# Order of Silu, Exp and Ln in the front stage of a three-layer Mamba block

## Chip, cores and metric

One core of a Trainium2 chip. The metric is the device time of one execution of the whole program in microseconds, the median of three runs.

## What is computed

A tower of token embedding with attention, a delta-rule attention block, two mixtures of experts and, between them, three Mamba layers beside an LSTM. The change is in the Mamba layers alone:

```
xz = einsum('bld,ed->ble', x, wi); xin, z = split(xz, 2)
u = silu(cb + conv4(xin, cw))
xdbl = einsum('blc,ec->ble', u, xpw)
dt_in, Bc, Cc = xdbl[..., :32], xdbl[..., 32:48], xdbl[..., 48:]
dt = softplus(einsum('blr,cr->blc', dt_in, dw) + db)
A = -exp(Alog)
h = exp(dt_t * A) * h + (dt_t * u_t) * B_t      # scan over 128 steps
y = (h . C_t + u * Dp) * silu(z);  m = layernorm(m + y @ wo)
```

There are 16 sequences of 128 tokens, 256 channels and 16 states.

## The kernel before

The program is a row of stages, each a block in which the engines run their own lists of instructions and wait on semaphores; a barrier stands at the end of a block. Each Mamba layer has two blocks: `mamba_front_stage`, which makes u, gate, dt, dtu = dt * u and the B and C rows, and `mamba_scan_stage`, which runs 64 turns of decay, scan and accumulation (in layers 1 and 2 with one LSTM step in each turn). When a block ends, POOL alone clears its semaphores (`close_semaphores`, L39 to L45) before it starts on the next.

The front stage works on four groups of 512 columns (4 sequences). 256 channels are two halves of 128 partitions, so most tiles of a group are 128 partitions by 2x512. The order in each engine's list is written out by hand:

- PE: `turn` (transpose), `channels_in` and `gates_in` (input projection), `project` (x_proj, L1567), `step_in` (dt projection, one half at a time through one PSUM bank, L1574).
- ACT: `normal`, `turned`, `gate` (Silu from PSUM, L1357), `channels` (Silu, L1361), `projected` (two copies, L1365 and L1366), `step_input` (dt with its bias, L1370), and `logarithm` (L1372 on), which makes log(1 + exp(-|x|)): Abs L1375, Exp L1377, the small Exp of A_log with group 0, L1379, and Ln L1383. A change of function that needs another table is preceded by an ACT_TABLE_LOAD, which the compiler puts in.
- DVE: `statistics`, `mean_shift`, `convolve`, `split` (B and C into bf16 parts, L1462, CAST L1464, L1466), and `step_size`, five instructions of 128x1024: w = (e + 1) - 1 (L1472), e = w - e (L1475), l = (w > 0) * l (L1476), l = l - e (L1479), dt = max(x, 0) + l (L1481). w is what 1 + e keeps of e, so the sum is softplus with the lost bits of e added. In the first layer some one-off scalings for the LSTM (L1508 to L1514) stand ahead of the last step size, in all layers the sign of A (L1517).
- POOL: `inverse_root` and `step_times_input`, dtu = dt * u, one instruction of 128x1024 for each group (L1324), which waits for dt.
- SP: the C rows go to DRAM.

The tile `ln` and the tile `conv` have two buffers each, used by groups in turn; e lies in tile y, w in tile dtu.

```
dve.wait_ge(s["w_done"], g + 1)
dve.wait_ge(s["ln_done"], g + 1)
nc.vector.tensor_tensor(e, w, e, ALU.subtract).then_inc(s["diff_done"], 1)
```

Of the kernel before, what the change touches and what calls it, by code (L numbers as in the profile page):

```python
# [9 lines left out]
ALU = mybir.AluOpType  # L10
ACT = mybir.ActivationFunctionType
# [5 lines left out]
GROUPS = 4  # L17
# [1256 lines left out]
def mamba_front_stage(nc, io, m, z, r, layer):  # L1274
# [5 lines left out]
                            "e_done w_done ln_done a_exp a_done diff_done masked_done t_done dt_done dtu_done")  # L1280
    with ExitStack() as mem:
# [14 lines left out]
        def cols(g):  # L1296
            return slice(g * GT, (g + 1) * GT)
# [5 lines left out]
        with nc.Block() as block:  # L1303
# [12 lines left out]
            @block.gpsimd  # L1316
            def _(pool):
                def inverse_root(g):
                    pool.wait_ge(s["var_done"], g + 1)
                    nc.gpsimd.tensor_tensor(root[:, g, :], var[:, g, :], m.neg_half[:, 0:GS], ALU.pow).then_inc(s["root_done"], 1)  # L1320

                def step_times_input(g):
                    pool.wait_ge(s["dt_done"], g + 1)
                    nc.gpsimd.tensor_tensor(z["dtu"][:, :, cols(g)], z["dt"][:, :, cols(g)], z["u"][:, :, cols(g)], ALU.mult).then_inc(s["dtu_done"], 1)  # L1324

                for g in range(GROUPS):
                    inverse_root(g)
                if first:
                    nc.gpsimd.memset(r["hs"][:, 0:1, :], 0.0)
                    nc.gpsimd.memset(r["cell"][:, :], 0.0).then_inc(s["cleared"], 1)  # L1330
                    pool.wait_ge(s["cleared"], 1)
                for g in range(GROUPS):
                    step_times_input(g)
                pool.wait_ge(s["dtu_done"], GROUPS)

            @block.scalar
            def _(act):
# [34 lines left out]
                def logarithm(g):  # L1372
                    e = z["y"][:, :, cols(g)]
                    act.wait_ge(s["x_done"], HALVES * (g + 1))
                    nc.scalar.activation(e, z["dt"][:, :, cols(g)], ACT.Abs).then_inc(s["abs_done"], 1)  # L1375
                    act.wait_ge(s["abs_done"], g + 1)
                    nc.scalar.activation(e, e, ACT.Exp, scale=-1.0).then_inc(s["e_done"], 1)  # L1377
                    if g == 0:
                        nc.scalar.activation(z["a"][:, :, :], z["a_log"][:, :, :], ACT.Exp).then_inc(s["a_exp"], 1)  # L1379
                    act.wait_ge(s["e_done"], g + 1)  # L1380
                    if g >= 2:
                        act.wait_ge(s["dt_done"], g - 1)
                    nc.scalar.activation(ln[:, g % 2], e, ACT.Ln, bias=m.ones_col[:, 0:1]).then_inc(s["ln_done"], 1)  # L1383
# [21 lines left out]
                logarithm(0)  # L1405
                channels(2)
                gate(3)
                step_input(1, 0)
                channels(3)
                step_input(1, 1)  # L1410
                projected(2)
# [3 lines left out]
                step_input(2, 1)  # L1415
                logarithm(2)
                step_input(3, 0)
                step_input(3, 1)
                logarithm(3)

            @block.vector
            def _(dve):
# [45 lines left out]
                def step_size(g):  # L1468

                    e, w, l, x = z["y"][:, :, cols(g)], z["dtu"][:, :, cols(g)], ln[:, g % 2], z["dt"][:, :, cols(g)]  # L1470
                    dve.wait_ge(s["e_done"], g + 1)
                    nc.vector.tensor_scalar(w, e, 1.0, -1.0, ALU.add, ALU.add).then_inc(s["w_done"], 1)  # L1472
                    dve.wait_ge(s["w_done"], g + 1)
                    dve.wait_ge(s["ln_done"], g + 1)
                    nc.vector.tensor_tensor(e, w, e, ALU.subtract).then_inc(s["diff_done"], 1)  # L1475
                    nc.vector.scalar_tensor_tensor(out=l, in0=w, scalar=0.0, in1=l, op0=ALU.is_gt, op1=ALU.mult).then_inc(s["masked_done"], 1)  # L1476
                    dve.wait_ge(s["masked_done"], g + 1)
                    dve.wait_ge(s["diff_done"], g + 1)
                    nc.vector.tensor_tensor(l, l, e, ALU.subtract).then_inc(s["t_done"], 1)  # L1479
                    dve.wait_ge(s["t_done"], g + 1)  # L1480
                    nc.vector.scalar_tensor_tensor(out=x, in0=x, scalar=0.0, in1=l, op0=ALU.max, op1=ALU.add).then_inc(s["dt_done"], 1)  # L1481
# [18 lines left out]
                convolve(3)  # L1500
                step_size(0)
                split(2)
                step_size(1)
                split(3)
                step_size(2)
# [11 lines left out]
                nc.vector.tensor_scalar(z["a"][:, :, :], z["a"][:, :, :], -1.0, None, ALU.mult).then_inc(s["a_done"], 1)  # L1517
                step_size(3)
                dve.wait_ge(s["a_done"], 1)
# [7 lines left out]
            def _(pe):  # L1527
# [69 lines left out]
                channels_in(3)  # L1597
                gates_in(3)
                step_in(1, 0)
                project(2)  # L1600
# [1643 lines left out]
```

## Time and profile before

| | us |
|---|---|
| median of 3 runs (lowest, highest) | 2222.15 (2221.86, 2230.19) |
| the profiled execution, its own time | 2218.03 |
| its span | 2216.2 |
| busy: PE / DVE / ACT / POOL | 1795.8 / 1491.5 / 1081.9 / 1121.8 |
| front stages, from first to last work | about 1006 to 1084, 1301 to 1388, 1628 to 1707 |
| scan stages | about 1084 to 1301, 1388 to 1628, 1707 to 1945 |

The span is the time from the first to the last instruction of the profiled execution; all times of the trace count from its start. The busy times are sums over the whole program, so what an engine bounds in one stage is not read from them. In a timeline each row is one instruction, or several alike in a row (x2), with its start, its duration and, in brackets, how long its engine sat idle before it and what it waited for. From the start of one row to the start of the next is what an instruction costs its engine: it may be a little less than the duration, since the next one overlaps, or a little more, where the next one waits for its result.

### The profile page before, as it was taken

The page shows a single profiled execution, that of the slowest core. Times are in us where ns is not written, and L with a number is a line of the kernel's source. Part 1 is how long each engine was busy: PE and PEld are TensorE (multiplying, and loading weights), DVE is VectorE, ACT ScalarE, POOL GpSimd, SP SyncE. Part 2 cuts the span into 40 slices and gives each one's busy share as a digit, 9 for nine tenths or more (in the row PEclk, how much of TensorE's full clock was granted, in tenths as well). Part 3 has the DMA queues.
Part 4 walks back from the last instruction along what each step waited for, and adds up shares of the span by engine and source line. Part 5 has one row for each costly group of instructions (what it writes and reads, how often), then busy time and mean ns, then how long its engine had stood idle before and what let it go on. Part 6 is the DMA issues. An engine that isn't in the chain of part 4 may idle for free. (4 is left out here: it accounts for less than half of the span.)

```text
span 2216.2 us, 39566 instructions
## 1 busy us (share of the span) xinstructions
PE 1795.8 (81%) x13962; PEld 1146.5 (52%) x13962; DVE 1491.5 (67%) x2798; ACT 1081.9 (49%) x2732; POOL 1121.8 (51%) x1094
## 2 busy tenths in 40 slices
PE   7986799999976789766477785999984999975990
PEld 4554467767665569742122241566641666643550
DVE  4657877777623412247799968899967899955552
ACT  3662256666643424325666647555546455541110
POOL 4100656555580220051499951899922899924005
PEclk9997899999987579988699997899995899987995
DMA  8000111111111048410132200332201222203662
GB/s 298 14 1 8 43 33 35 29 40 40 40 33 27 19 136 220 135 34 19 44 86 81 81 24 3 79 84 77 76 3 23 68 77 77 68 17 94 193 180 66
DMA packets 196552, 149.91 MB, mean 68 GB/s; under 512 B 93393, under 2 KB 155687, under 8 KB 194838
## 3 DMA queue, kind: packets, MB, share of 16 engines
q1 hardware_dynamic: 191766, 138.74, 22.5%
q0 software_dynamic: 4608, 8.86, 1.4%
q8 instruction: 104, 1.70, 0.3%
q14 instruction: 74, 0.61, 0.1%
HBM read 108.93 MB, written 39.19 MB: 67 GB/s over the span
## 5 line engine op out<-in xcount | busy, mean ns | idle before, releaser
L1685 POOL TENSOR_TENSOR mc_hc<-mc_states,mc_c_sb 128x1024 f32<-128x1024 f32 x192 | 451.4, 2351 | 40.5 <-DVE mc_states L1778 29.5
L1778 DVE TENSOR_TENSOR_SCAN mc_states<-psum,mc_dbu 128x512 f32<-128x512 f32 x384 | 459.9, 1217 | 13.0 <-POOL mc_dbu L1675 7.9
L1816 PE MATMUL psum<-mc_hc,ident 128*128 128x512 f32 x768 | 421.3, 644 | 49.4 <-POOL mc_hc L1685 46.7
L1696 ACT ACTIVATE psum<-dt,a 128x508 f32<-128x508 f32 x384 | 261.3, 686 | 18.3 <-DVE mc_states L1778 17.0
L815 POOL TENSOR_TENSOR fw_tmp<-zeros 128x30 f32<-128x30 f32 (+14 forms) x240 | 127.0, 529 | 201.7 <-DMA zeros<-fw_blocks 183.5
L1675 POOL TENSOR_TENSOR mc_dbu<-dtu,mc_b_sb 128x384 f32<-128x384 f32 x192 | 191.4, 998 | 10.6 <-remote 7.0
L1816 PEld LDWEIGHTS psum<-mc_hc,ident 128*128 128x128 f32 x768 | 122.6, 193 | 108.4 <-POOL mc_hc L1685 68.1
L853 ACT ACTIVATE fw_U<-psum 32x128 f32<-32x128 f32 x440 | 118.1, 269 | 97.1 <-PE psum L1114 49.9
L1764 DVE TENSOR_TENSOR mc_dbu<-psum,dtu 128x640 f32<-128x640 f32 x192 | 154.0, 802 | 7.0 <-PE psum L1796 6.7
L1703 ACT ACTIVATE mc_b_sb<-psum 128x192 f32<-128x192 f32 x192 | 63.5, 331 | 170.6 <-PE psum L1802 170.1
L819 POOL TENSOR_TENSOR zeros<-zeros,fw_tmp 128x30 f32<-128x30 f32 (+14 forms) x240 | 131.3, 547 | 18.8
L2001 POOL DMA_INDIRECT c_y<-slots_y,slots x32 | 30.3, 948 | 152.7 <-issue 152.7
L2001 POOL DMA_INDIRECT f_y<-slots_y,slots x32 | 31.2, 974 | 149.5 <-issue 149.5
L1324 POOL TENSOR_TENSOR dtu<-dt,u 128x1024 f32<-128x1024 f32 x12 | 28.1, 2342 | 152.5 <-DVE dt L1481 152.5
L1096 PE MATMUL psum<-fw_qkT 64*128 64x128 f32 x1024 | 79.7, 298 | 27.3 <-DVE fw_A L1025 26.4
L2450 ACT ACTIVATE e_up<-psum,e_b 128x256 f32<-128x256 f32 x128 | 56.7, 474 | 84.3 <-PE psum L2495 84.3
L1096 PEld LDWEIGHTS psum<-fw_qkT 64*128 64x128 f32 x1024 | 66.7, 199 | 41.3 <-DVE fw_A L1025 29.4
L1848 PEld LDWEIGHTS psum<-ls_parts,mc_half_ident 128*128 128x128 f32 x256 | 49.4, 197 | 72.9 <-DVE ls_parts L1770 56.2
L3012 ACT ACTIVATE e_act<-psum 64x256 f32<-64x256 f32 x64 | 24.2, 377 | 125.4 <-PE psum L3057 125.4
L1834 PE MATMUL psum<-ls_hs,ls_whh 64*64 64x16 f32 x2048 | 85.3, 212 | 0.0
L1802 PE MATMUL psum<-bc,select 96*128 96x192 bf16 x192 | 48.9, 255 | 44.9 <-PEq L1303 43.7
L2460 DVE TENSOR_SCALAR e_xT<-psum,x_gb 128x256 f32<-128x256 f32 x32 | 17.4, 544 | 94.8 <-PE psum L2488 94.8
(439 smaller groups left out, 4120.0 us busy)
## 6 DMA issues: line engine op xcount, KB each, us to landing
mc_c_sb<-c_rows SPq DMA_DIRECT2D x192, 256.0 KB, 3.2
e_w<-in_L_ffn_ew SPq DMA_DIRECT2D x64, 256.0 KB, 3.2
slots_x<-zeros SPq DMA_DIRECT2D x12, 1024.0 KB, 14.5
e_x<-slots_x SPq DMA_DIRECT2D x96, 128.0 KB, 2.3
slots_y<-e_y SPq DMA_DIRECT2D x96, 128.0 KB, 2.0
e_w<-in_L_ffn_w SPq DMA_DIRECT2D x64, 128.0 KB, 2.2
fw_blocks<-fw_A SPq DMA_DIRECT2D x128, 32.0 KB, 1.7
zeros<-fw_blocks SPq DMA_DIRECT2D x8, 512.0 KB, 3.7
```

Of the source, the lines that this page charges most:

```text
L815: nc.gpsimd.tensor_tensor(part, z[:, u + 1:BLK, u:u + 1].to_broadcast([P, rows, u]), z[:, u:u + 1, 0:u].to_broadcast([P, rows, u]), ALU.mu ...
L819: nc.gpsimd.tensor_tensor(z[:, u + 1:BLK, 0:u], z[:, u + 1:BLK, 0:u], part, ALU.subtract).then_inc(s["subtracted"], 1)
L853: last = nc.scalar.activation(U[BLK * i:BLK * (i + 1), 2 * r:2 * r + 2, :], RU8[place(i, r), 2 * r:2 * r + 2, :], ACT.Copy)
L1096: last = nc.tensor.matmul(S[h % 2][:, h // 2, :], qkT[lo:lo + DH, 1, h // 2, :], qkT[lo:lo + DH, k, h // 2, :], start=True, stop=True)
L1675: nc.gpsimd.tensor_tensor(dbu[:, k % 2, :, SPLIT:GT], z["dtu"][:, :, c * GT + SPLIT:(c + 1) * GT], b_sb[:, k % 2, :].unsqueeze(1).to_broad ...
L1685: nc.gpsimd.tensor_tensor(hc[:, k % 2], states[:, k % 2], c_sb[:, k % AHEAD, :].unsqueeze(1).to_broadcast([P, HALVES, GT]), ALU.mult).then ...
L1696: nc.scalar.activation(decay4[:, f, :, 1:P], z["dt"][:, f, cols].rearrange("p (b t) -> p b t", b=GS)[:, :, 1:P], ACT.Exp, scale=z["a"][:, ...
L1703: nc.scalar.activation(b_sb[:, k % 2, :], rest_ps, ACT.Copy).then_inc(s["b_copied"], 1)
L1764: nc.vector.tensor_tensor(dbu[:, k % 2, :, 0:SPLIT], b_ps[k % 2][:, 0:SPLIT].unsqueeze(1).to_broadcast([P, HALVES, SPLIT]), z["dtu"][:, :, ...
L1778: nc.vector.tensor_tensor_scan(out=states[:, k % 2, f, :], data0=decay_ps[:, f, :], data1=dbu[:, k % 2, f, :], initial=0.0, op0=ALU.mult, ...
L1816: last = nc.tensor.matmul(y_ps[:, f, :], m.ident, hc[:, k % 2, f, :], start=(n == 0), stop=(n == NSTATE - 1), skip_group_check=True)
L1834: last = nc.tensor.matmul(step_ps[rows, q * BATCH:(q + 1) * BATCH], r["whh"][rows, q, rows], hs[rows, first_step + k, :], start=False, sto ...
```

## The change

On ACT the function `logarithm` is cut into `magnitude` (Abs), `exponential` and `logarithm` (Ln alone). The Silus of groups 2 and 3 and the copies of group 2 stand ahead of the first Exp. Exp of groups 0 and 1 follow one another, with the small Exp behind, then Ln of 0 and 1. Groups 2 and 3 keep Exp and Ln each. At the end a table load for the scan's Exp is issued.

On DVE `step_size` is cut into `step_base` (w, w - e, max(x, 0) - (w - e)), which needs Exp alone, and `step_size` (mask of Ln and the sum). The sum is taken in another order; w - e goes to the tile conv, so it also waits for the last Silu that reads it. On POOL the last product is cut: POOL does the first half, DVE the second, with a wait for dt. On PE `project(2)` moves ahead of `gates_in(3)`.

```
-                def logarithm(g):
+                def magnitude(g):
+                    act.wait_ge(s["x_done"], HALVES * (g + 1))
+                    nc.scalar.activation(z["y"][:, :, cols(g)], z["dt"][:, :, cols(g)], ACT.Abs).then_inc(s["abs_done"], 1)
+
+                def exponential(g):
                     e = z["y"][:, :, cols(g)]
-                    act.wait_ge(s["x_done"], HALVES * (g + 1))
-                    nc.scalar.activation(e, z["dt"][:, :, cols(g)], ACT.Abs).then_inc(s["abs_done"], 1)
                     act.wait_ge(s["abs_done"], g + 1)
                     nc.scalar.activation(e, e, ACT.Exp, scale=-1.0).then_inc(s["e_done"], 1)
-                    if g == 0:
-                        nc.scalar.activation(z["a"][:, :, :], z["a_log"][:, :, :], ACT.Exp).then_inc(s["a_exp"], 1)
+
+                def logarithm(g):
                     act.wait_ge(s["e_done"], g + 1)
...
                 step_input(0, 1)
-                logarithm(0)
+                magnitude(0)
                 channels(2)
+                projected(2)
                 gate(3)
                 step_input(1, 0)
                 channels(3)
+                exponential(0)
                 step_input(1, 1)
-                projected(2)
+                magnitude(1)
+                exponential(1)
+                nc.scalar.activation(z["a"][:, :, :], z["a_log"][:, :, :], ACT.Exp).then_inc(s["a_exp"], 1)
+                logarithm(0)
                 logarithm(1)
                 step_input(2, 0)
                 projected(3)
                 step_input(2, 1)
+                magnitude(2)
+                exponential(2)
                 logarithm(2)
                 step_input(3, 0)
                 step_input(3, 1)
+                magnitude(3)
+                exponential(3)
                 logarithm(3)
+                nc.scalar.preload_act_table_set("exp_and_others")
...
+                def step_base(g):
+                    e, w, x = z["y"][:, :, cols(g)], z["dtu"][:, :, cols(g)], z["dt"][:, :, cols(g)]
+                    diff = conv[:, g % 2].rearrange("p f j c -> p f (j c)")
                     dve.wait_ge(s["e_done"], g + 1)
                     nc.vector.tensor_scalar(w, e, 1.0, -1.0, ALU.add, ALU.add).then_inc(s["w_done"], 1)
                     dve.wait_ge(s["w_done"], g + 1)
+                    dve.wait_ge(s["u_done"], GROUPS)
+                    if g >= 2:
+                        dve.wait_ge(s["base_done"], g - 1)
+                    nc.vector.tensor_tensor(diff, w, e, ALU.subtract).then_inc(s["diff_done"], 1)
+                    dve.wait_ge(s["diff_done"], g + 1)
+                    nc.vector.scalar_tensor_tensor(out=x, in0=x, scalar=0.0, in1=diff, op0=ALU.max, op1=ALU.subtract).then_inc(s["base_done"], 1)
+
+                def step_size(g):
+                    w, l, x = z["dtu"][:, :, cols(g)], ln[:, g % 2], z["dt"][:, :, cols(g)]
                     dve.wait_ge(s["ln_done"], g + 1)
-                    nc.vector.tensor_tensor(e, w, e, ALU.subtract).then_inc(s["diff_done"], 1)
                     nc.vector.scalar_tensor_tensor(out=l, in0=w, scalar=0.0, in1=l, op0=ALU.is_gt, op1=ALU.mult).then_inc(s["masked_done"], 1)
                     dve.wait_ge(s["masked_done"], g + 1)
-                    dve.wait_ge(s["diff_done"], g + 1)
-                    nc.vector.tensor_tensor(l, l, e, ALU.subtract).then_inc(s["t_done"], 1)
-                    dve.wait_ge(s["t_done"], g + 1)
-                    nc.vector.scalar_tensor_tensor(out=x, in0=x, scalar=0.0, in1=l, op0=ALU.max, op1=ALU.add).then_inc(s["dt_done"], 1)
+                    dve.wait_ge(s["base_done"], g + 1)
+                    nc.vector.tensor_tensor(x, x, l, ALU.add).then_inc(s["dt_done"], 1)
+
+                def last_step_times_input():
+                    dve.wait_ge(s["dt_done"], GROUPS)
+                    c = cols(GROUPS - 1)
+                    nc.vector.tensor_tensor(z["dtu"][:, 1, c], z["dt"][:, 1, c], z["u"][:, 1, c], ALU.mult).then_inc(s["dtu_last"], 1)
...
                 convolve(3)
+                split(2)
+                step_base(0)
                 step_size(0)
-                split(2)
+                step_base(1)
                 step_size(1)
                 split(3)
+                step_base(2)
                 step_size(2)
...
+                step_base(3)
                 step_size(3)
+                last_step_times_input()
...
                 channels_in(3)
+                project(2)
                 gates_in(3)
                 step_in(1, 0)
-                project(2)
```

On ACT, first layer, from the Abs of group 0 (y is the tile of e, mf_ln the tile of Ln, u takes the Silu of the convolution, zeros and bc the two copies). Before:

```order
L1375 ACTIVATE y<-dt 128x2x512
L1377 ACT_TABLE_LOAD
L1377 ACTIVATE y<-y 128x2x512
L1379 ACTIVATE a<-ma_log 128x32
L1383 ACT_TABLE_LOAD
L1383 ACTIVATE mf_ln<-y,ones_col 128x1024
L1361 ACT_TABLE_LOAD
L1361 ACTIVATE u<-mf_conv 128x2x512
L1357 ACTIVATE gate<-psum 128x512 x2
L1370 ACTIVATE dt<-psum,mdb 128x512
L1361 ACTIVATE u<-mf_conv 128x2x512
L1370 ACTIVATE dt<-psum,mdb 128x512
```

And now:

```order
L1376 ACTIVATE y<-dt 128x2x512
L1363 ACTIVATE u<-mf_conv 128x2x512
L1367 ACTIVATE zeros<-psum 64x512
L1368 ACTIVATE bc<-psum 32x512
L1359 ACTIVATE gate<-psum 128x512 x2
L1372 ACTIVATE dt<-psum,mdb 128x512
L1363 ACTIVATE u<-mf_conv 128x2x512
L1381 ACT_TABLE_LOAD
L1381 ACTIVATE y<-y 128x2x512
L1372 ACTIVATE dt<-psum,mdb 128x512
L1376 ACTIVATE y<-dt 128x2x512
L1381 ACTIVATE y<-y 128x2x512
```

The three loads between Abs and the Silus of groups 2 and 3 are now one, behind both Silus, and the second Exp follows the first without a load.

On DVE, first layer, from the step size of group 0 to that of group 1 (dtu holds w, mf_conv now the difference). Before:

```order
L1472 TENSOR_SCALAR dtu<-y 128x2x512
L1475 TENSOR_TENSOR y<-dtu,y 128x2x512
L1476 SCALAR_TENSOR_TENSOR mf_ln<-dtu,mf_ln 128x1024
L1479 TENSOR_TENSOR mf_ln<-mf_ln,y 128x1024
L1481 SCALAR_TENSOR_TENSOR dt<-dt,mf_ln 128x2x512
L1462 TENSOR_TENSOR mf_rest<-psum,bc 32x512
L1464 CAST bc<-mf_rest 32x512
L1466 TENSOR_TENSOR bc<-mf_rest,bc 32x512
L1472 TENSOR_SCALAR dtu<-y 128x2x512
L1475 TENSOR_TENSOR y<-dtu,y 128x2x512
```

And now:

```order
L1476 TENSOR_TENSOR mf_rest<-psum,bc 32x512
L1478 CAST bc<-mf_rest 32x512
L1480 TENSOR_TENSOR bc<-mf_rest,bc 32x512
L1488 TENSOR_SCALAR dtu<-y 128x2x512
L1493 TENSOR_TENSOR mf_conv<-dtu,y 128x1024
L1495 SCALAR_TENSOR_TENSOR dt<-dt,mf_conv 128x2x512
L1500 SCALAR_TENSOR_TENSOR mf_ln<-dtu,mf_ln 128x1024
L1503 TENSOR_TENSOR dt<-dt,mf_ln 128x2x512
L1488 TENSOR_SCALAR dtu<-y 128x2x512
L1493 TENSOR_TENSOR mf_conv<-dtu,y 128x1024
L1495 SCALAR_TENSOR_TENSOR dt<-dt,mf_conv 128x2x512
```

The split of group 2 (mf_rest, bc) stands ahead of the first step size instead of behind it, and the step sizes of groups 0 and 1 follow one another with nothing between them.

## Rows read from the trace of the kernel before

**Rows 1.** The page, costliest groups: line engine op tiles | busy us, mean ns | idle us before
```profile
L1324 POOL TENSOR_TENSOR dtu<-dt,u 128x1024 f32<-128x1024 f32 x12 | 28.1, 2342 | 152.5 <-DVE dt L1481 152.5
```

**Rows 2.** Timeline of ACT, first layer: start us, us, engine line op, tiles, shapes [idle before]
```profile
1036.12 0.69 ACT L1370 ACTIVATE dt<-psum,mdb 128x512 f32<-128x512 f32 x1
1036.83 1.06 ACT L1375 ACTIVATE y<-dt 128x1024 f32<-128x1024 f32 x1
1037.91 1.28 ACT L1377 ACT_TABLE_LOAD   x1
1039.20 1.06 ACT L1377 ACTIVATE y<-y 128x1024 f32<-128x1024 f32 x1
...
1040.40 1.28 ACT L1383 ACT_TABLE_LOAD   x1
1041.69 1.15 ACT L1383 ACTIVATE mf_ln<-y,ones_col 128x1024 f32<-128x1024 f32 x1
1042.86 1.28 ACT L1361 ACT_TABLE_LOAD   x1
...
1045.11 1.07 ACT L1357 ACTIVATE gate<-psum 128x512 f32<-128x512 f32 x2
...
1075.04 1.15 ACT L1383 ACTIVATE mf_ln<-y,ones_col 128x1024 f32<-128x1024 f32 x1
```

**Rows 3.** Timeline of DVE, first layer, step size of group 0
```profile
1044.16 0.68 DVE L1472 TENSOR_SCALAR dtu<-y 128x1024 f32<-128x1024 f32 x1
1044.88 1.23 DVE L1475 TENSOR_TENSOR y<-dtu,y 128x1024 f32<-128x1024 f32 x1
1046.02 1.22 DVE L1476 SCALAR_TENSOR_TENSOR mf_ln<-dtu,mf_ln 128x1024 f32<-128x1024 f32 x1
1047.27 1.22 DVE L1479 TENSOR_TENSOR mf_ln<-mf_ln,y 128x1024 f32<-128x1024 f32 x1
1048.53 1.23 DVE L1481 SCALAR_TENSOR_TENSOR dt<-dt,mf_ln 128x1024 f32<-128x1024 f32 x1
```

**Rows 4.** The same timeline at the end of the stage, DVE and POOL
```profile
1079.94 1.23 DVE L1481 SCALAR_TENSOR_TENSOR dt<-dt,mf_ln 128x1024 f32<-128x1024 f32 x1
...
1081.25 2.34 POOL L1324 TENSOR_TENSOR dtu<-dt,u 128x1024 f32<-128x1024 f32 x1 [7.05 <-DVE dt L1481]
```

**Rows 5.** Timeline of PE around x_proj; windows row: us, five engines busy, PEclk, DMA share, GB/s
```profile
1032.08 1.93 PE L1567 MATMUL psum<-u,mxw 128*64 128x512 f32 x4
...
1045.26 3.41 PE L1567 MATMUL psum<-u,mxw 128*64 128x512 f32 x4 [4.10 <-ACT u L1361]
...
1045.20:1071.00 25.80, 15.02 (x18) 3.38 (x18) 19.82 (x20) 20.31 (x25) 4.69 (x2) 0.63 0.01 3
```

**Rows 6.** Instructions by line over the span: duration ns min/median/max, first and last start
```profile
L1464 DVE CAST bc<-mf_rest x12: 414/414/1956, 1028.8 to 1686.8; 32x512 bf16<-32x512 f32 x12
...
L1510 DVE TENSOR_SCALAR ls_whh<-ls_whh x4: 214/219/2387, 1071.8 to 1074.3; 128x128 f32<-128x128 f32 x4
...
L1032 DVE TENSOR_TENSOR fw_qk<-fw_qk,fw_rz x32: 1224/1226/2453, 179.2 to 603.3; 128x1024 f32<-128x1024 f32 x32
```

**Rows 7.** Timeline of DVE and POOL, first layer, split of group 3 and the one-off scalings
```profile
1062.45 0.68 DVE L1462 TENSOR_TENSOR mf_rest<-psum,bc 32x512 f32<-32x512 f32 x1
...
1065.88 0.69 DVE L1472 TENSOR_SCALAR dtu<-y 128x1024 f32<-128x1024 f32 x1
...
1071.69 0.15 DVE L1508 TENSOR_TENSOR ls_bsum<-mf_bias 128x4 f32<-128x4 f32 x1
...
1074.80 0.68 DVE L1472 TENSOR_SCALAR dtu<-y 128x1024 f32<-128x1024 f32 x1
...
1062.50 2.34 POOL L1324 TENSOR_TENSOR dtu<-dt,u 128x1024 f32<-128x1024 f32 x1 [10.26 <-DVE dt L1481]
```

**Rows 8.** Timeline of POOL and DVE at the start of the first scan
```profile
1086.93 1.95 POOL L1675 TENSOR_TENSOR mc_dbu<-dtu,mc_b_sb 128x384 f32<-128x384 f32 x2 [3.35 <-remote]
...
1088.02 2.34 DVE L1778 TENSOR_TENSOR_SCAN mc_states<-psum,mc_dbu 128x512 f32<-128x512 f32 x2 [2.43 <-POOL mc_dbu L1675]
```

More of the change, by code:

```diff
@@ L1279, in mamba_front_stage @@
                             "in_mm gate_done taps conv_done u_done dbl_mm rows_done hi_done rest_done mid_done split_done rows_out dt_mm x_done abs_done "
-                            "e_done w_done ln_done a_exp a_done diff_done masked_done t_done dt_done dtu_done")
+                            "e_done w_done ln_done a_exp a_done diff_done base_done masked_done dt_done dtu_done dtu_last")
     with ExitStack() as mem:
@@ L1320, in inverse_root, with step_times_input @@
                     nc.gpsimd.tensor_tensor(root[:, g, :], var[:, g, :], m.neg_half[:, 0:GS], ALU.pow).then_inc(s["root_done"], 1)
-                def step_times_input(g):
+                def step_times_input(g, halves=range(HALVES)):
                     pool.wait_ge(s["dt_done"], g + 1)
-                    nc.gpsimd.tensor_tensor(z["dtu"][:, :, cols(g)], z["dt"][:, :, cols(g)], z["u"][:, :, cols(g)], ALU.mult).then_inc(s["dtu_done"], 1)
+                    f = slice(halves.start, halves.stop)
+                    nc.gpsimd.tensor_tensor(z["dtu"][:, f, cols(g)], z["dt"][:, f, cols(g)], z["u"][:, f, cols(g)], ALU.mult).then_inc(s["dtu_done"], 1)
                 for g in range(GROUPS):
@@ L1331, in _ @@
                     pool.wait_ge(s["cleared"], 1)
-                for g in range(GROUPS):
+                for g in range(GROUPS - 1):
                     step_times_input(g)
+                step_times_input(GROUPS - 1, range(1))
                 pool.wait_ge(s["dtu_done"], GROUPS)
@@ L1382, in logarithm @@
                         act.wait_ge(s["dt_done"], g - 1)
-                    nc.scalar.activation(ln[:, g % 2], e, ACT.Ln, bias=m.ones_col[:, 0:1]).then_inc(s["ln_done"], 1)
+                    nc.scalar.activation(ln[:, g % 2], z["y"][:, :, cols(g)], ACT.Ln, bias=m.ones_col[:, 0:1]).then_inc(s["ln_done"], 1)
                 if not first:
@@ L1466, in split @@
                     nc.vector.tensor_tensor(z["bc"][64:96, g, :], rest[:, g % 2, :], z["bc"][0:32, g, :], ALU.subtract).then_inc(s["split_done"], 1)
-                def step_size(g):
-                    e, w, l, x = z["y"][:, :, cols(g)], z["dtu"][:, :, cols(g)], ln[:, g % 2], z["dt"][:, :, cols(g)]
+                def step_base(g):
+                    e, w, x = z["y"][:, :, cols(g)], z["dtu"][:, :, cols(g)], z["dt"][:, :, cols(g)]
+                    diff = conv[:, g % 2].rearrange("p f j c -> p f (j c)")
                     dve.wait_ge(s["e_done"], g + 1)
@@ L1473, in step_size @@
                     dve.wait_ge(s["w_done"], g + 1)
+                    dve.wait_ge(s["u_done"], GROUPS)
[6 more added lines that the diff above has]
+                    w, l, x = z["dtu"][:, :, cols(g)], ln[:, g % 2], z["dt"][:, :, cols(g)]
                     dve.wait_ge(s["ln_done"], g + 1)
-                    nc.vector.tensor_tensor(e, w, e, ALU.subtract).then_inc(s["diff_done"], 1)
                     nc.vector.scalar_tensor_tensor(out=l, in0=w, scalar=0.0, in1=l, op0=ALU.is_gt, op1=ALU.mult).then_inc(s["masked_done"], 1)
                     dve.wait_ge(s["masked_done"], g + 1)
-                    dve.wait_ge(s["diff_done"], g + 1)
-                    nc.vector.tensor_tensor(l, l, e, ALU.subtract).then_inc(s["t_done"], 1)
-                    dve.wait_ge(s["t_done"], g + 1)
-                    nc.vector.scalar_tensor_tensor(out=x, in0=x, scalar=0.0, in1=l, op0=ALU.max, op1=ALU.add).then_inc(s["dt_done"], 1)
+                    dve.wait_ge(s["base_done"], g + 1)
[4 more added lines that the diff above has]
+                    nc.vector.tensor_tensor(z["dtu"][:, 1, c], z["dt"][:, 1, c], z["u"][:, 1, c], ALU.mult).then_inc(s["dtu_last"], 1)
+                    dve.wait_ge(s["dtu_last"], 1)
                 dve.wait_ge(m.front_loaded, FRONT_LOADS * (layer + 1))
```

## Prediction

> **What bounds the kernel now.** The change touches one stage that runs three times, the front of each recurrent layer, between the scans. Read first the page's group of the product dt times u on POOL [rows 1]: twelve instructions of 2.34 us, with 152.5 us of idle time in front of them, all of it waiting for dt from DVE. POOL is last in this stage and is fed by DVE. Then read the timeline of ACT, first layer [rows 2]. The reader is to see the table loads: Exp and Ln stand behind different tables, a Silu behind a third, and each load takes 1.28 us. From the start of Abs (1036.83) to Silu's load (1042.86) is 6.0 us, and the pattern is repeated for groups 1 to 3. Start-to-start steps I use: dt to Abs 0.71, Abs to the next 1.08, load to activation 1.29, Exp to the next 1.0 (its 1.06 less the overlap), Exp with the small Exp behind it 1.20. The last Ln starts at 1075.04 and ends at 1076.19. Then the timeline of DVE [rows 3]: a step size is five instructions of 1024 columns, started 0.72, 1.14, 1.25 and 1.26 us apart. Its second waits for Ln, so four instructions stand behind the last Ln. The last of them starts at 1079.94 and ends at 1081.17, and POOL's last product runs 1081.25 to 1083.59 [rows 4]. The end of the stage is therefore ACT's chain to the last Ln (1076.19), then 7.4 us of DVE and POOL. ACT is the bound, and DVE has slack in front of each Ln.
>
> Times below are those of the first layer; I price the other two by the same chain.
>
> **The change on ACT.** Three of the nine loads ahead of a stage's last Ln go: the Silus of groups 2 and 3 now stand ahead of the first Exp, and two Exps share one load, as do two Lns. The step sizes of group 0 come later for it. Up to 1037.91 nothing moves. Then, by steps from [rows 2]: Silu of group 2 ends at 1039.0. TensorE's x_proj for group 2 follows at once, 1.93 us if its clock is still up [rows 5], so ACT copies at 1041.1, does two copies and two gate Silus at 0.5 to 0.6 each (a pair of Silus takes 1.07), and waits for the dt matmul behind the gates' four matmuls (1040.95 + 1.93 + 1.0 = 1043.9). dt 0.6, Silu of group 3 at 1044.5, load at 1045.55, first Exp at 1046.85, dt at 1047.85, Abs at 1048.55, second Exp at 1049.65, load at 1050.85 behind the small Exp, first Ln at 1052.1. It ends at 1053.25; the masking on DVE starts 0.1 later, at 1053.35. Before it started at 1046.02, so the first step size is 7.3 us later. From there on ACT runs 3.3 us ahead of its old time: the last Ln ends at 1072.9.
>
> **The change on DVE.** Five instructions remain five, of the same sizes. Three of them (w, the difference, the base) no longer need Ln, and two follow it. If ACT stayed the bound, 1.25 + 1.22 us and half a product would stand behind the last Ln, and the end would be near 1076.7, 6.9 us earlier. But DVE has no slack left after 1053.35. It then owes five-instruction groups of 5.5 us (0.72 + 1.25 + 1.14 + 1.25 + 1.14) for groups 1 to 3, and the split of group 3.
>
> **Who blocks whom.** The question is what POOL's products of groups 0 to 2 do to a DVE that never rests. They have always run; what is new is that nothing covers them. The trace shows the price [rows 6]: the CAST of the split takes 0.414 us and once per layer or so 1.956, when a product runs beside it. One of four 128x128 scalings takes 2.387 instead of 0.22, and it was the second of four back to back: POOL had come in between two DVE instructions that were both ready. The multiplication at L1032, both inputs in SBUF, takes 1.224 or up to 2.453 while POOL works. L1462, with one input in PSUM, took 0.68 beside a product [rows 7]. So I take every DVE instruction with two SBUF inputs, and the fast one-input ones, as blocked for a whole product. That is a step beyond the rows, since no row has a SCALAR_TENSOR_TENSOR of this shape beside POOL. Bounds for one product: 0 (only the fast ones are blocked, and none is met) and 2.39. I take 2.2 for groups 0 and 2 in the later layers, since DVE's next instructions are all of the blocked kind.
>
> On this the Trainium skill (SBUF — State Buffer, Who interferes with whom) says that a Vector instruction with two SBUF inputs contends with a GpSimd instruction that reads SBUF, and that the second to issue blocks until the first is done. The trace agrees for TENSOR_TENSOR (1.224 to 2.453); for the two SCALAR_TENSOR_TENSOR of each group no row here shows it. By the page the sum is the one below; without it, it would be the first rival's.
>
> **The sum, first layer.** Masking 1053.35, dt of group 0 at 1054.6, w of group 1 at 1055.75. POOL asks at 1055.9 and gets in behind w: +2.15. dt of group 1 then at 1062.3. Split with its CAST blocked: 1.25 from dt, then 3.43 to the next w [rows 7] (1.89 without the block of 1.54); w of group 2 at 1067.0, dt at 1071.35. Then the one-off scalings of the first layer, 3.11 us, blocked as before, so w of group 3 at 1075.6, its dt at 1079.95 to 1081.2. The last product: DVE's half 0.68 (512 columns, as L1462), POOL's half 1.27 (on the line through 0.98 for 384 and 2.34 for 1024 columns [rows 1, 8]; half of 2.34 is the lower bound). Both have two SBUF inputs, so they come one behind the other: 1081.2 + 0.68 + 1.27 = 1083.15. Gain 0.4 us.
>
> **Second and third layer.** No one-off scalings, but the product of group 2 blocks two-input work of group 3: w at 1072.6, +2.2, dt at 1079.2 to 1080.4, halves to 1082.4. Gain 1.2 each. In the third the old end is some half a microsecond late, which I add: 1.7.
>
> **The load at the end of the stage.** It takes 1.28 off the scan's start on ACT. I cost it at nothing: the first scan waits for POOL's first mc_dbu (1086.93, ends 1087.9), and DVE starts at 1088.02 [rows 8]. POOL is late, 3.35 us idle, because it first clears the stage's 40 semaphores. There is one more now, at most 0.08 us (3.35 over 40), three times: -0.2. In front, the load stands behind the last Ln with 8 us to spare. The moved x_proj and the split of group 2 are hidden in the wait for the first Exp.
>
> Sum: 0.4 + 1.2 + 1.7 - 0.2 = **3.1 us faster**, against the profiled execution's 2218.0. The median of the three runs shown is 2222.15, 4 above it; I subtract from the median: **2219.0**. A measurement of this kernel can tell about 0.5% (11 us) from no change, so this is no change.
>
> **Rivals.**
> 1. *Only the fast one-input instructions are blocked.* For: the clearest blocked rows are of that kind. Against: L1032's 2.453. Then the first product costs nothing, and the last halves run side by side. First layer: dt of group 3 at 1077.75, end 1080.4, gain 3.2; in the others 4.0 if w of group 3 meets the product, 6.2 if not and ACT becomes the bound again. Sum 11.2 to 16, time 2206 to 2211. Chance 0.15.
> 2. *TensorE falls to its lower clock before x_proj of group 2; slower.* It does x_proj in 1.93 after steady work and in 3.41 after 4.1 us of idling, and was granted 0.63 of the full clock on average from 1045.2 to 1071 [rows 5], so part of that time at 1.2 and part at 2.4 GHz. In the new order x_proj, the gates and the dt matmul stand ahead of the first Exp. Slow, they cost 1.5 + 1.5 + 0.9 = 3.9 us on the way to the first Ln, and DVE pays all of it: 3 x 3.9 - 3.1 = 8.6 us slower, 2231, and beyond 0.5% only with another microsecond in each layer. It decides as soon as the first masking starts more than 1 us after 1053.35. Against: the gap before x_proj is only 0.6 us, since Silu comes at once. Chance 0.04.
> 3. *ACT stays the bound*, POOL's products slip into gaps: end near 1076.7 in each layer, 20 us, 2202. It needs 5 us of slack on DVE that I don't find. Chance 0.03.
>
> The forecast keeps 0.78; its own range, with a block of 0 to 2.4 us at each of the two new places, is 2213 to 2224. To hold the time 8 times in 10 I stretch down to part of rival 1: 2209 to 2224. Faster by over 0.5% (below 2211) has rivals 1 and 3, 0.17; slower by over 0.5% is the worse half of rival 2, 0.02; no change 0.81.
>
> **What would show it.** Right: the difference of group 1 takes 3.4 us instead of 1.23; the masking of group 0 starts 16 to 17 us after the Abs of group 0; from there no idle time on DVE until the end; ACT's last Ln ends 3 us earlier with 8 us of idling behind it; the halves lie one behind the other; the scan's first DVE instruction still waits for mc_dbu. Wrong: step-size instructions at 1.22 beside running products, DVE waiting for a later Ln, or x_proj of group 2 at 3.4 us.

## The result, and the profile after

The changed kernel takes 2218.22 us (median of 20 runs, 2212.54 to 2225.24), the kernel before 2223.43 in the same comparison (20 runs, 2217.94 to 2230.19). The ratio is 0.9973 with a 95% interval of 0.9962 to 0.9985: 3.3 to 8.4 us less, inside the 0.5% that the prediction called no change. The predicted 3.1 us would be a ratio of 0.9986, just outside that interval: the sign and the class were right, the size somewhat low. Ratios leave out executions over 1.5% longer than the fastest of the same kernel, in which TensorE's granted clock was lower; here there were none.

The profiled execution says the opposite at first sight: its span is 2218.6 us against 2216.2 before. So the change is read where it was made, as the time from the first Abs of a layer (ACT) to DVE's first instruction in that layer's scan stage. Layers are counted from 1 here and below, so the LSTM steps run in the scans of layers 2 and 3.

| us, layers 1 / 2 / 3 | front, first Abs to the scan stage | from there to the first scan |
|---|---|---|
| before | 47.28 / 47.26 / 47.73 | 3.90 / 4.19 / 4.19 |
| after | 46.42 / 45.43 / 45.43 | 4.27 / 4.27 / 4.27 |
| gain | 0.86 / 1.83 / 2.30 | -0.37 / -0.08 / -0.08 |

That is 4.99 us in front and 0.53 given back, 4.5 us in all, and it lies within the measured 3.3 to 8.4. What hides it in the profiled execution lies in stages with the same code in both kernels; a part below comes back to it.

POOL's group on the page, against [rows 1] (152.5 us idle, waiting for dt):

```profile
L1325 POOL TENSOR_TENSOR dtu<-dt,u 128x1024 f32<-128x1024 f32 (+1 forms) x12 | 28.4, 2366 | 147.3 <-DVE dt L1503 147.3
```

It is still the one that waits last, by 5.2 us less; the second form is the half. The timeline of ACT, first layer, answers to [rows 2]. This Abs starts at 1042.62 instead of 1036.83, so 5.79 us are to be taken off before times are compared.

```profile
1042.62 1.06 ACT L1376 ACTIVATE y<-dt 128x1024 f32<-128x1024 f32 x1
1043.58 1.04 ACT L1363 ACTIVATE u<-mf_conv 128x1024 f32<-128x1024 f32 x1
1046.64 0.59 ACT L1367 ACTIVATE zeros<-psum 64x512 f32<-64x512 f32 x1 [2.02 <-PE psum L1601]
...
1051.25 1.28 ACT L1381 ACT_TABLE_LOAD   x1
1052.55 1.06 ACT L1381 ACTIVATE y<-y 128x1024 f32<-128x1024 f32 x1
...
1057.79 2.19 ACT L1387 ACTIVATE mf_ln<-y,ones_col 128x1024 f32<-128x1024 f32 x2
...
1076.68 1.15 ACT L1387 ACTIVATE mf_ln<-y,ones_col 128x1024 f32<-128x1024 f32 x1
1077.84 1.28 ACT L1433 ACT_TABLE_LOAD   x1
1089.01 0.18 ACT L1752 ACTIVATE psum<-dt 128x8 f32<-128x8 f32 x1 [9.89 <-PEq L1303]
```

The reader is to see one load ahead of the first Exp, both first Lns as one row, and 9.89 us of idling behind the last load: ACT no longer sets the end. Its last Ln starts 34.06 us after the Abs, where it was 38.21. DVE and POOL in the same stretch, against [rows 3, 4, 7]:

```profile
1053.64 0.69 DVE L1488 TENSOR_SCALAR dtu<-y 128x1024 f32<-128x1024 f32 x1 [1.73 <-ACT y L1381]
1054.36 1.23 DVE L1493 TENSOR_TENSOR mf_conv<-dtu,y 128x1024 f32<-128x1024 f32 x1
1055.62 1.22 DVE L1495 SCALAR_TENSOR_TENSOR dt<-dt,mf_conv 128x1024 f32<-128x1024 f32 x1
1058.97 1.23 DVE L1500 SCALAR_TENSOR_TENSOR mf_ln<-dtu,mf_ln 128x1024 f32<-128x1024 f32 x1 [2.12 <-ACT mf_ln L1387]
...
1062.09 3.26 DVE L1493 TENSOR_TENSOR mf_conv<-dtu,y 128x1024 f32<-128x1024 f32 x1
...
1069.75 1.95 DVE L1478 CAST bc<-mf_rest 32x512 bf16<-32x512 f32 x1
...
1078.04 2.78 DVE L1542 TENSOR_SCALAR ls_whh<-ls_whh 128x128 f32<-128x128 f32 x4
...
1085.44 1.23 DVE L1503 TENSOR_TENSOR dt<-dt,mf_ln 128x1024 f32<-128x1024 f32 x1
1086.69 0.69 DVE L1509 TENSOR_TENSOR dtu<-dt,u 128x512 f32<-128x512 f32 x1
...
1061.60 2.66 POOL L1325 TENSOR_TENSOR dtu<-dt,u 128x1024 f32<-128x1024 f32 x1 [32.38 <-DVE dt L1503]
...
1086.74 1.77 POOL L1325 TENSOR_TENSOR dtu<-dt,u 128x512 f32<-128x512 f32 x1 [6.27 <-DVE dt L1503]
```

From the masking at 1058.97 to the half at 1086.69 no DVE row has idle time in front. Inside that stretch three rows are longer than their work: the difference of group 1 (3.26 for 1.23), the CAST (1.95 for 0.41) and the scalings (2.78 for four of 0.22), each beside a product of POOL. The last two rows of each engine show the halves one behind the other: POOL asks at 1086.74 while DVE's half runs until 1087.38, and ends at 1088.51, that is 1.13 after it. In layer 2 the difference of group 3 is the one blocked:

```profile
1382.14 3.24 DVE L1493 TENSOR_TENSOR mf_conv<-dtu,y 128x1024 f32<-128x1024 f32 x1
...
1395.66 1.22 DVE L1812 TENSOR_TENSOR_SCAN mc_states<-psum,mc_dbu 128x512 f32<-128x512 f32 x1 [1.29 <-POOL mc_dbu L1709]
```

The second row is the first scan: it waits for POOL's mc_dbu, as in [rows 8], and not for ACT.

### The profile page after: what moved, and what is told of

It is laid out like the page before. It is cut to its first block and busy times, and to the rows that moved or that the text cites. A ratio compares the mean times of both kernels' runs of the same rounds, so it can differ in the third digit from the quotient of the medians.

```text
span 2218.6 us, 39564 instructions
## 1 busy us (share of the span) xinstructions
PE 1797.8 (81%) x13962; PEld 1150.1 (52%) x13962; DVE 1499.9 (68%) x2801; ACT 1069.6 (48%) x2723; POOL 1121.1 (51%) x1094
## 5 line engine op out<-in xcount | busy, mean ns | idle before, releaser
L1325 POOL TENSOR_TENSOR dtu<-dt,u 128x1024 f32<-128x1024 f32 (+1 forms) x12 | 28.4, 2366 | 147.3 <-DVE dt L1503 147.3
```

## Experiments

Two questions were open. *Theory*: DVE's own work is the bound from the first masking on, and POOL's products block it, whichever instruction with two SBUF inputs is next. *Rival*: only the fast one-input instructions are blocked, or the wait for Ln still sets the end. The second question is which part of the change carries the gain. The three front times given with each run are those of one profiled execution; they repeat from kernel to kernel within 0.02 us where nothing was changed. The whole program moves by more than that for other reasons: the first four kernels below took 2233.75, 2223.26, 2204.88 and 2245.25 us beside 2221.25 for the kernel before, the one with w ahead 2229.08 beside a median of 2221.91, and the remaining three 2374.29 to 2376.36 on a chip where the median of the kernel before was 2309.68.

**The last product whole, on POOL.**

```
-                for g in range(GROUPS - 1):
+                for g in range(GROUPS):
                     step_times_input(g)
-                step_times_input(GROUPS - 1, range(1))
...
-                last_step_times_input()
+                dve.wait_ge(s["dt_done"], GROUPS)
```

> The changed kernel with its last product whole on POOL again. I read the front stage from its first Abs (ACT) to the first DVE instruction of the scan: 47.29, 47.26 and 47.73 us before the change, 46.42, 45.42 and 45.43 with it. My theory (the two halves come one behind the other, 0.69 on DVE and then POOL's, 3.07 us from the start of the last dt): POOL whole takes 1.3 + 2.34 = 3.64, so each stage is 0.6 us longer, about 47.0, 46.0 and 46.0. Rival (the halves run side by side, so cutting saves a full half, 1.1 to 1.2 us): 47.6, 46.6 and 46.6.

Measured 47.02 / 46.02 / 46.00. The halves are worth 0.6 us in each layer: from the start of the last sum to the end of POOL's product it is 3.65 us here and 3.07 with halves. Side by side they would have been worth half a product.

**Without the table load at the end** (the line with `preload_act_table_set` taken out).

> The changed kernel without the table load at the end of the front stage; the compiler puts the load ahead of the scan's first Exp again. My theory (the first scan waits for POOL's first mc_dbu): ACT's first Exp of the scan is 1.3 us later, the first scan on DVE starts at the same distance from the first DVE instruction of its stage, 3.9 to 4.3 us. Rival (the load on ACT is on the path): that distance grows by 0.5 to 1.3 us in each of three layers.

Measured 46.43 / 45.44 / 45.44, and 4.27 / 4.26 / 4.26 on to the first scan. The load moves into the scan stage and changes neither number: it was worth nothing, since POOL's mc_dbu comes last there.

**The products of groups 0 to 2 left out.**

```
-                for g in range(GROUPS - 1):
-                    step_times_input(g)
                 step_times_input(GROUPS - 1, range(1))
-                pool.wait_ge(s["dtu_done"], GROUPS)
+                pool.wait_ge(s["dtu_done"], 1)
```

> The changed kernel without POOL's products of groups 0 to 2 (dtu keeps w there, so part of the computation is left out); the last product stays as it is. My theory (DVE is the bound and each product costs it 2.0, 1.5 and 2.0 to 2.4 us): the front stage from first Abs to the first DVE instruction of the scan falls from 46.4, 45.4, 45.4 to about 40.5, 40.1, 40.1, where ACT's last Ln begins to bound; the difference of group 1 takes 1.23 us and the CAST of the split 0.41. Rival (ACT bounds or the products are hidden): unchanged within 0.5 us.

Measured 41.72 / 40.77 / 40.76, 4.7 us less in each layer, where 5.9 and 5.3 had been expected. The computation is not complete in this kernel, so it is a measurement of the cost only. All twelve differences are now at 1.23:

```profile
L1491 DVE TENSOR_TENSOR mf_conv<-dtu,y x12: 1224/1226/1227, 1049.4 to 1683.8; 128x1024 f32<-128x1024 f32 x12
...
1071.39 0.69 DVE L1486 TENSOR_SCALAR dtu<-y 128x1024 f32<-128x1024 f32 x1 [0.91 <-ACT y L1379]
```

In layer 1 the three blocks of the changed kernel are 2.03 + 1.54 + 2.15 = 5.7 us; they vanish, and 0.91 comes back as a wait for ACT's Exp of group 3 (0.82 in layer 2). So the price of POOL's products is shown, and so is the next bound: once they are gone, DVE is ready for group 3 a little less than a microsecond before ACT has its Exp.

**All four products on DVE.**

```
+                def times_input(g):
+                    dve.wait_ge(s["dt_done"], g + 1)
+                    nc.vector.tensor_tensor(z["dtu"][:, :, cols(g)], z["dt"][:, :, cols(g)], z["u"][:, :, cols(g)], ALU.mult).then_inc(s["dtu_done"], 1)
...
                 step_size(0)
+                times_input(0)
```

> The changed kernel with all four products on DVE (128x1024, behind each step size) and none on POOL. My theory: DVE pays 1.25 us for a product in place of being blocked for 2.0, 1.5 and 2.0 to 2.4, and 1.25 + 1.23 behind the last dt in place of 3.07: 2.7 us less in the first layer, 2.5 in the others, so 43.7, 42.9 and 42.9 us from first Abs to the scan. Rival (more work on the engine that bounds, while POOL had taken it off: DVE gains only the blocked time that the trace shows on the difference and pays four products): 5.0 us of products against 5.5 of blocking, no change within 0.7 us.

Measured 44.20 / 43.07 / 43.07: 2.2 to 2.4 us less than the changed kernel, although DVE has 4 x 1.23 us more to do and lost only its half of 0.69. So the rival, no change within 0.7 us, falls; the expected 43.7, 42.9 and 42.9 were missed by 0.5 and 0.2. A product costs DVE about 1.25 us when it does it itself. When POOL does it beside DVE, it costs 2.03 on a difference, 1.54 on the CAST and 2.15 on the scalings. The program's own time was long here, 2245.25 us, from a stage that the edit doesn't touch. Windows of the second mixture's experts in this kernel, then in the changed one (us, five engines busy, PEclk, DMA share, GB/s):

```profile
2060.00:2100.00 40.00, 40.00 (x111) 21.30 (x110) 11.86 (x33) 3.83 (x11) 0.00 (x0) 0.50 0.36 107
```

```profile
2070.00:2110.00 40.00, 40.00 (x200) 23.49 (x199) 21.50 (x60) 7.54 (x20) 0.00 (x0) 1.00 0.68 194
```

TensorE is busy throughout in both, but at 0.50 it does 111 matmuls in 40 us instead of 200. That is why single totals were not used to judge a microsecond.

**The base of group 1 ahead of the step size of group 0.**

```
                 step_base(0)
-                step_size(0)
                 step_base(1)
+                step_size(0)
                 step_size(1)
```

> The changed kernel with one line moved on DVE: the base of group 1 ahead of the step size of group 0. In the changed kernel DVE sits idle for 2.12 us until the first Ln is there, with the second Exp long done. My theory (everything behind the first Ln is one unbroken chain of DVE): those 2.1 us come off the end of every layer, from first Abs to the scan about 44.2, 43.2 and 43.2 us in place of 46.42, 45.43 and 45.43; POOL's first product now falls behind a masking and blocks the sum of group 1, which takes about 3.2 us. Rival (the start of the chain does not set the end, ACT or POOL does): within 0.5 us of the changed kernel.

Measured 44.23 / 43.49 / 43.24. DVE fills the 2.12 us wait for the first Ln with group 1's three instructions, and about that much comes off in layers 1 and 3. In layer 2 ACT is late once: DVE waits 0.42 us for the Exp of group 3, and its w is then the one that a product blocks (2.46 us for 0.69). The block then falls on the sum of group 1:

```profile
1105.07 1.22 DVE L1500 SCALAR_TENSOR_TENSOR mf_ln<-dtu,mf_ln 128x1024 f32<-128x1024 f32 x1
1106.32 3.25 DVE L1503 TENSOR_TENSOR dt<-dt,mf_ln 128x1024 f32<-128x1024 f32 x1
...
1105.30 3.19 POOL L1325 TENSOR_TENSOR dtu<-dt,u 128x1024 f32<-128x1024 f32 x1 [33.94 <-DVE dt L1503]
```

POOL's row begins at 1105.30 and is 3.19 long instead of 2.34: it is 0.85 us longer, about what the running masking still takes (0.99 us). It gets in when that ends, and the sum behind it waits for all of the product.

**The old sum in the new order** (the four instructions behind Ln as before, the halves kept).

```
-                    nc.vector.tensor_tensor(diff, w, e, ALU.subtract).then_inc(s["diff_done"], 1)
...
                     dve.wait_ge(s["ln_done"], g + 1)
+                    nc.vector.tensor_tensor(e, w, e, ALU.subtract).then_inc(s["diff_done"], 1)
...
+                    nc.vector.tensor_tensor(l, l, e, ALU.subtract).then_inc(s["t_done"], 1)
```

> The changed kernel with the old sum: orders of ACT, PE and of the splits as changed, last product in halves, but step_size as before, four instructions behind each Ln. My theory (DVE works through from the first Ln on; the new sum helps by what it does before the first Ln and nowhere else): dt of group 0 is 2.4 us later and so is the end of every stage, 48.8, 47.8 and 47.8 us from first Abs to the scan, more than before the change (47.3). Rival (the new sum has its worth at the last Ln, where two instructions in place of four are on the path): the same 2.4 only if ACT bounds there; else the end moves by nothing. Both give the end; apart they are told by the idle time of DVE in front of the last group's second instruction: 0 by my theory, over 1 us by the rival.

Measured 48.89 / 47.88 / 47.88, slower than the kernel before. DVE has as many instructions of the same length, but now stands idle in front of the first Ln with nothing to do:

```profile
1090.73 0.69 DVE L1486 TENSOR_SCALAR dtu<-y 128x1024 f32<-128x1024 f32 x1 [1.73 <-ACT y L1381]
1096.13 1.23 DVE L1489 TENSOR_TENSOR y<-dtu,y 128x1024 f32<-128x1024 f32 x1 [4.71 <-ACT mf_ln L1387]
```

4.71 us against 2.12. Beside the new order the new sum is worth 2.45 us in each layer, and it comes from this one wait, which is 2.59 us longer. Behind it no DVE row of the stage has idle time in front, in any layer. The rival wanted over 1 us of it in front of the last group's second instruction, so it falls.

**The old order on ACT and PE** (Silus behind the first Ln, split of group 2 behind the first step size; new sum, halves and load kept).

```
                 magnitude(0)
+                exponential(0)
...
+                logarithm(0)
                 channels(2)
-                projected(2)
...
-                project(2)
                 gates_in(3)
                 step_in(1, 0)
+                project(2)
```

> The new sum, the halves and the early load, with the order of ACT and PE as before the change (Exp and Ln of group 0 ahead of the Silus of groups 2 and 3, five more table loads' worth of ACT time than needed) and the split of group 2 behind the step size of group 0. My theory (the first Ln decides, not the number of loads): DVE starts its chain 5 us earlier, is blocked by products less, and ACT's last Ln, 3.3 us later than in the changed kernel, just begins to bound: about 44.9 us from first Abs to the scan in all three layers, less than with the Silus ahead (46.4, 45.4, 45.4). Rival (fewer loads are worth their time): 3 us more than the changed kernel, 49.4, 48.4 and 48.4.

Measured 45.71 / 45.36 / 45.53: 0.7 less than the changed kernel in layer 1, the same within 0.1 in the other two. The expected 44.9 was missed by 0.5 to 0.8. Three waits stand in the rows. ACT's dt waits 3.27 us for TensorE where it was 2.05 before. DVE's first difference waits for the last Silu, since it is written to the tile conv, so the first masking starts 13.37 us after the Abs, 3.0 us earlier than in the changed kernel and not the expected 5. And in front of group 3 DVE waits for ACT's Exp, the third row, from layer 2:

```profile
1098.83 0.69 ACT L1372 ACTIVATE dt<-psum,mdb 128x512 f32<-128x512 f32 x1 [3.27 <-PE psum L1608]
...
1095.65 1.22 DVE L1493 TENSOR_TENSOR mf_conv<-dtu,y 128x1024 f32<-128x1024 f32 x1 [2.96 <-ACT u L1363]
...
1424.58 0.69 DVE L1488 TENSOR_SCALAR dtu<-y 128x1024 f32<-128x1024 f32 x1 [3.24 <-ACT y L1381]
```

That last wait is 0.55 / 3.24 / 3.40 us in the three layers, where the changed kernel has none. It comes last, so with the old order ACT sets the end, and the earlier wait for the Silu is covered by it.

Against the kernel before it is a gain of 1.57 / 1.90 / 2.20. So the Silus ahead of Exp and Ln, the headline of the change, bring nothing beside this list of DVE's: they take three loads off ACT, put the masking of group 0 later on DVE (16.35 us after the Abs; 13.37 here, 9.19 before the change), and the bound passes from ACT to DVE at nearly the same end. What the old order would do beside a shorter list of DVE's was not run; an estimate follows at the last run.

**w of group 1 ahead of the step size of group 0**, so that the base, a SCALAR_TENSOR_TENSOR, is next when POOL gets in.

```
                 step_base(0)
+                kept(1)
                 step_size(0)
```

> The changed kernel with w of group 1 (0.69 us) made ahead of the step size of group 0, while DVE waits for the first Ln. POOL's first product then asks while the difference (TENSOR_TENSOR) runs, and the next instruction on DVE is the base of group 1, a SCALAR_TENSOR_TENSOR with two SBUF inputs: the kind of which no row of the kernel before shows that a product blocks it. My theory (blocked like the TENSOR_TENSOR): the base of group 1 takes about 3.2 us, POOL's record about 3.1, and only the 0.7 of w come off: 45.7, 44.7 and 44.7 us from first Abs to the scan. Rival (not blocked): the base takes 1.22 beside a product, and two more microseconds come off: 43.7, 42.7 and 42.7.

Measured 45.70 / 44.69 / 44.69. The base is blocked like the difference:

```profile
1064.64 1.22 DVE L1497 TENSOR_TENSOR mf_conv<-dtu,y 128x1024 f32<-128x1024 f32 x1
1065.89 3.25 DVE L1499 SCALAR_TENSOR_TENSOR dt<-dt,mf_conv 128x1024 f32<-128x1024 f32 x1
...
1064.87 3.19 POOL L1325 TENSOR_TENSOR dtu<-dt,u 128x1024 f32<-128x1024 f32 x1 [33.14 <-DVE dt L1507]
```

This settles the step that the prediction took beyond its rows. The 0.7 us gained is w itself, moved into the wait for Ln.

**Both: all products on DVE, and the base of group 1 ahead.** This was run twice, on two chips. On the first one every kernel took longer, and the mean granted clock of TensorE lay between 0.838 and 0.892, against 0.889 to 0.899 in those compared on the second (the kernel before took 2309.68 us on the first, median of 17 runs).

> All products on DVE and the base of group 1 ahead of the step size of group 0 together. The products alone gave 44.20, 43.07 and 43.07 us from first Abs to the scan. My theory: another 2.1 less, 42.1, 41.0 and 41.0, since ACT's last Ln would end the stage only at about 39.6. That is 18 us less than before the change over three layers, 0.8%: 2205 where before has 2223. Rival (ACT becomes the bound as soon as DVE is 1 us shorter): 43, 42 and 42. What the clock of TensorE does in the later stages comes on top: with the products on DVE alone, a later stage was 32 us longer at half clock; if that belongs to the order of work and not to the one run, it shows here too, and the whole program is slower than before.

> The kernel with all products on DVE and the base of group 1 ahead once more, since its first timing fell among executions of 2267 to 2383 us of the kernel before. My theory: 41.9, 40.9 and 40.9 us from first Abs to the scan wherever it runs, 18.6 us less than before the change over the three layers, 0.8% of 2223. Rival (the front stages' gain is given back later, by turns at the lower clock in the scans and by the last expert stage): a ratio within 0.5% of 1, with the longer stages to be seen in the trace.

Measured in front 41.98 / 40.86 / 41.14 and 41.99 / 40.84 / 41.14. The ratio to the kernel before was 0.9907 both times, with intervals of 0.9873 to 0.9941 and 0.9885 to 0.9930. On the second chip that is 2202.05 us against 2221.91 as medians of the 5 and 11 executions that the ratio takes. The second rival, a ratio within 0.5% of 1, lies outside both intervals, and the half clock in the expert stage does not belong to having the products on DVE: with them there, these five take 2198 to 2210 us. In the first layer:

```profile
1062.64 1.22 DVE L1496 SCALAR_TENSOR_TENSOR mf_ln<-dtu,mf_ln 128x1024 f32<-128x1024 f32 x1
1063.90 1.23 DVE L1499 TENSOR_TENSOR dt<-dt,mf_ln 128x1024 f32<-128x1024 f32 x1
1065.15 1.22 DVE L1503 TENSOR_TENSOR dtu<-dt,u 128x1024 f32<-128x1024 f32 x1
...
1078.80 0.62 DVE L1538 TENSOR_SCALAR ls_whh<-ls_whh 128x128 f32<-128x128 f32 x4
...
1085.30 1.23 DVE L1503 TENSOR_TENSOR dtu<-dt,u 128x1024 f32<-128x1024 f32 x1
```

In this layer, from w of group 0 (1056.39) to the last product, DVE has no idle time and no instruction longer than its work. ACT is now close behind: in layer 3 DVE waits 0.20 us for the Exp of group 3. So this is where the Silus ahead should be worth having. With ACT's old order group 3 could begin 37.39 us after the Abs (layer 2 of the run with that order), and from there to the scan it is 7.39 us here, which makes about 44.8 us in place of 40.84. That is an estimate from the rows of two kernels; no run has both. This is the version to keep: 18 us off the kernel before by the front stages (5.3 + 6.4 + 6.6), against 5.0 for the change as made.

**Why the profiled execution isn't shorter.** At the first Abs the changed kernel is already 5.79 us late, by stages that have the same code in both: DVE's first instruction behind the token stage starts at 161.83 us before and at 164.03 after, and at 164.8 to 168.6 in the kernels above that ran at a like clock. Against this stand the 4.5 us gained. Behind the last scan another 1.4 us are lost, again in unchanged stages. The scans vary too. Windows at the start of the second and third layer's scans, before and after:

```profile
1392.00:1417.00 25.00, 24.20 (x172) 15.99 (x172) 22.23 (x33) 12.12 (x39) 20.46 (x14) 0.77 0.35 83
...
1711.00:1736.00 25.00, 24.21 (x133) 15.85 (x134) 17.08 (x24) 9.29 (x31) 15.29 (x11) 0.53 0.30 69
```

```profile
1396.00:1421.00 25.00, 23.36 (x128) 15.20 (x129) 17.16 (x26) 9.16 (x28) 15.31 (x10) 0.54 0.25 67
...
1711.00:1736.00 25.00, 19.66 (x134) 13.09 (x135) 17.98 (x30) 10.36 (x33) 16.14 (x11) 0.63 0.26 80
```

Behind these windows the clock is 1.00 until 1600 and 1900 in both kernels. While it is down, some turns of the scan take 5.8 to 6.3 us, where most take 3.3 to 3.8. Before, the 64 turns took 221.6 us in layer 2 (no such turn) and 227.7 in layer 3 (two of them); after, 227.8 (two) and 221.7 (none), which cancels by luck. In the kernel with the last product whole it was 233.2 and 227.5, in the one without the load 230.7 and 221.7. The same code thus takes 221.6 to 233.2, by steps of about 3 us. Whether the length of the front stage has a part in how many turns are slow is open; no run was made for it.

## Why the prediction was right, and where its sizes were off

- *DVE becomes the bound and the first step size comes later.* Right. The masking of group 0 starts 16.35 us after the Abs, predicted 16.52; the 2.12 us in front of it are the last idle time. What the prediction says of the pattern on ACT before the change is loose in one point: the Exp and Ln loads come again in groups 1 to 3, the Silu load doesn't. Its count of nine loads is right.
- *Who blocks whom.* Right at each place named: the difference of group 1 took 3.26 (predicted 3.4), the CAST and the scalings as before, in layers 2 and 3 the difference of group 3. On the Trainium skill's rule (SBUF — State Buffer, Who interferes with whom) for Vector instructions with two SBUF inputs, the trace now agrees for SCALAR_TENSOR_TENSOR also, 3.25 against 1.22. Rival 1 falls by that, and leaving the products out shows that they cost 4.7 us in each layer.
- *Rival 2.* x_proj of group 2 took 1.93 us, 0.50 us after the engine went idle; the granted clock from 1043.6 to 1052.5 was 1.00. *Rival 3.* ACT idles 9.89 us at the end, and DVE never waits for a later Ln.
- *The halves.* One behind the other, as predicted; from the start of the last sum to POOL's end 3.07 us, predicted 3.20. POOL's half ends 1.13 us behind DVE's, less than the 1.17 that the prediction took as the least; its 1.27 also comes out as 1.25 on its own line.
- *The load at the end and the semaphores.* The load was worth nothing, as costed. The term of 0.08 us for one more semaphore held in layers 2 and 3; in layer 1 the scan starts 0.37 later. POOL's idle time ahead of mc_dbu is 3.71 there instead of 3.35; why this is 0.36 stays open. The number of semaphores is not the reason: with the same 41, and no product on POOL, layer 1 has 3.66 us from the front to the first scan, while layers 2 and 3 have 4.26 or 4.27 in every kernel with 41.
- *The mis-sized terms.* The gains were 0.86 / 1.83 / 2.30, predicted 0.4 / 1.2 / 1.7. In layer 1 the sum is 0.43 us too long: 0.17 at the masking, 0.13 at the halves, and 0.13 between, mostly the block, taken as 2.15 and measured as 2.03. In layers 2 and 3 the second block (2.2 taken, 2.02 measured) adds 0.2. All are of one sign. For the blocks the reason is that each was taken as nearly a whole product; the masking and the halves have reasons of their own (the Silu behind the Abs starts after 0.96 us and not after 1.08, and the halves as above).
- *The total, and some luck.* 2219.0 was predicted and 2218.22 measured. That the two are 0.8 apart is luck in part: 5.2 us came off where 3.1 were forecast, and the kernel before is 1.3 us higher in this comparison than the median from which the prediction subtracted. The prediction's own range of 2213 to 2224 doesn't follow from its bounds either: blocks of 0 and of 2.39 us at both places would give about 2208 and 2220.
- *What the text did not see.* It made ACT's last Ln 3.3 us earlier by the three loads saved (4.15 measured in layer 1), but did not ask what DVE would do with ACT's old order. With the order of before, the new sum and the halves gain 5.7 us in front instead of 5.0; the new order with the old sum loses 2.4. ACT's lead can be worth something only when DVE's list is shorter.

## What to carry to other kernels

When a change frees the engine that bounds a stage, price the next engine with the instructions that block it, not with its busy time: here POOL's products cost the stage 4.7 us a layer by what they made DVE wait, and moving these onto the busier engine made the stage shorter. Work that needs only the earlier of two results belongs ahead of the wait for the later one; beside the new order that brought 2.45 us a layer. Fewer table loads brought nothing beside this DVE, since ACT's time stopped being the bound; by the estimate above they are worth something again once DVE's list is cut. And where a clock or a latency chain elsewhere moves the total by steps of 3 us, compare the stage, not the total.

## What the hardware showed that was not expected

- POOL, once it waits, gets in between two DVE instructions that stand back to back: POOL's row began 0.2 us into a running DVE instruction, lasted 3.19 us instead of 2.34, and the next DVE instruction took 3.25. Each waited for the one that had asked before it, so a DVE list without a gap gives no protection: the instruction behind the running one pays for the whole product.
- A 128x1024 product costs DVE 1.25 us, and on POOL beside a DVE without slack 1.54 to 2.15 us of DVE's time, by what DVE does next. One more semaphore to clear between two blocks costs 0.07 to 0.08 us in layers 2 and 3 (4.19 against 4.27).
- The same expert stage ran at a granted clock of 0.50 in one execution and 1.00 in another, 111 against 200 matmuls in 40 us.
